# Feed-forward input through the 'A' bank, output and z transposes one slot sooner

## What is computed

```python
x = x + attn_a(_layernorm(x))   # 16 heads of 8, rotary, layer norm on q and k, softmax over all 256 keys
x = x + ffn(_layernorm(x))      # token-shift feed-forward
x = x + attn_b(_layernorm(x))   # windowed attention and one gradient step of a memory MLP
x = x + ffn(_layernorm(x))
```

```python
xr = mu_r * x + (1.0 - mu_r) * x_prev       # x_prev: x one token earlier
xk = mu_k * x + (1.0 - mu_k) * x_prev
r = sigmoid(xr @ W_r.T)
out = r * (square(relu(xk @ W_k.T)) @ W_v.T)
```

## Time and profile before

| | us |
|---|---|
| median of 3 runs | 1365.89 (1365.3 to 1366.46) |
| the profiled execution, time | 1367.37 |
| the profiled execution, span from first to last instruction | 1365.6 |
| TensorE busy | 1284.8 (94%) |
| VectorE busy | 1122.7 (82%) |
| ScalarE busy | 901.9 (66%) |
| GpSimd busy | 504.9 (37%) |

### The profile page before, as it was taken

One profiled execution on the slowest core, in us unless ns is written; L12 is line 12 of the kernel. 1 busy time (PEld: TensorE's weight loads), 2 busy tenths in 40 slices (PEclk: granted clock), 3 DMA queues, 4 the chain that ended last, 5 costly groups with the idle time before them and its releaser, 6 DMA issues.

```text
span 1365.6 us, 32982 instructions
## 1 busy us (share of the span) xinstructions
PE 1284.8 (94%) x10579; PEld 852.4 (62%) x10579; DVE 1122.7 (82%) x2849; ACT 901.9 (66%) x2504; POOL 504.9 (37%) x815
## 2 busy tenths in 40 slices
PE   7889999999999999888999999999999998999996
PEld 5445555555555555545566666666666665888885
DVE  5888999999999999876888888888888875778786
ACT  3278888888888888876565566556655653555563
POOL 5446666666666666533111111111111100232322
PEclk9999999999999999999999999999999999999998
DMA  2222332223333323210100010000000001232220
GB/s 80 77 76 81 82 79 76 73 78 80 82 91 103 99 69 84 67 51 17 32 28 29 28 49 28 30 28 28 27 30 25 20 17 41 79 87 82 85 86 27
DMA packets 101963, 79.61 MB, mean 58 GB/s; under 512 B 13780, under 2 KB 95124, under 8 KB 101796
## 3 DMA queue, kind: packets, MB, share of 16 engines
q1 hardware_dynamic: 100820, 76.99, 20.0%
q10 hardware_dynamic: 976, 0.54, 0.2%
HBM read 49.70 MB, written 27.79 MB: 57 GB/s over the span
## 4 chain that ended last, share of the span: by engine, by line
PE 49%; issue 1%; DVE 1%; ACT 1%; POOL 0%; POOLq 0%; DVEq 0%; ACTq 0%
PE b_psZ L1410 4%; PE b_psD L1331 4%; PE b_psZ L1342 4%; PE b_g L1394 4%; PE d_psO L1954 4%; PE b_g L1381 4%; PE d_psH L1946 4%; PE b_psM L1443 2%; PE b_psR L1387 2%; PE b_psL L1372 2%; PE b_psR L1403 2%; PE b_psD L1433 2%; PE b_psM L1455 1%; PE d_psG L1972 1%; PE d_psV L1985 1%
## 5 line engine op out<-in xcount | busy, mean ns | idle before, releaser
L790 DVE TENSOR_REDUCE a_MX<-a_psS 128x4 f32<-128x1024 f32 x248 | 303.2, 1223 | 44.6 <-PE a_psS L304 41.2
L591 ACT ACTIVATE a_PT<-a_psE 128x512 f32<-128x512 f32 x504 | 275.1, 604 | 59.3 <-PE a_psE L321 56.4
L1811 POOL TENSOR_TENSOR b_SWB<-b_b2col,b_SW 128x128 f32<-128x128 f32 x65 | 38.8, 597 | 346.2 <-ACT b_SW L1526 346.2
L335 PE MATMUL a_psV<-a_PT,a_VX 128*32 128x256 f32 x2048 | 137.0, 385 | 0.2 <-ACT a_PT L591 0.2
L1545 ACT ACTIVATE b_TH<-b_psZ 128x512 f32<-128x512 f32 x65 | 38.9, 598 | 128.7 <-PE b_psZ L1342 124.3
L304 PE MATMUL a_psS<-a_KS,a_QS 48*128 48x256 f16 x992 | 97.7, 275 | 22.1 <-DVE a_MX L790 20.6
L321 PE MATMUL a_psE<-a_QS,a_KS 50*128 50x256 bf16 x1008 | 97.5, 270 | 3.1 <-ACT a_PT L591 3.1
L1565 ACT ACTIVATE b_PR<-b_psL,b_mx 128x128 f32<-128x128 f32 x260 | 93.1, 369 | 0.9
L304 PEld LDWEIGHTS a_psS<-a_KS,a_QS 48*128 48x128 bf16 x992 | 29.1, 94 | 103.1 <-issue 48.2
L335 PEld LDWEIGHTS a_psV<-a_PT,a_VX 128*32 128x32 f32 x2048 | 53.4, 109 | 50.5 <-issue 27.5
L1693 DVE SCALAR_TENSOR_TENSOR b_HH<-b_TH,b_psZ 128x512 f32<-128x512 f32 x65 | 44.8, 689 | 44.1 <-ACT b_TH L1545 44.0
(11 more groups left out here) (298 smaller groups left out, 3426.4 us busy)
## 6 DMA issues: line engine op xcount, KB each, us to landing
a_KS<-kparts SPq DMA_DIRECT2D x63, 192.0 KB
a_QS<-qparts SPq DMA_DIRECT2D x126, 96.0 KB
qparts<-a_QP SPq DMA_DIRECT2D x64, 96.0 KB, 2.2
a_X<-x_in SPq DMA_DIRECT2D x32, 128.0 KB, 2.3
kparts<-a_KP SPq DMA_DIRECT2D x64, 64.0 KB, 2.1
x<-a_X SPq DMA_DIRECT2D x32, 128.0 KB, 1.8
b_X<-x SPq DMA_DIRECT2D x32, 128.0 KB, 2.2
zT<-b_XT SPq DMA_DIRECT2D x32, 128.0 KB, 1.7
```

Of the source, the lines that this page charges most:

```text
L335: mm = nc.tensor.matmul(psV[32 * h:32 * h + 32, 0:T], VX[:, b % UV, kt, at:at + 32], PT[:, gg, kt, h, :], start=(gg == 0 and kt == 0), sto ...
L591: nc.scalar.activation(PT[:, g % 2, :, h + s, :], shifted_bank(b, p, s), ACT.Exp).then_inc(S["exp"], 1)
L790: nc.vector.reduce_max(MX[:, b % 2, :].rearrange("q (s n) -> q s n", s=2)[:, :, 2 * p:2 * p + 2], score_banks(b, p)[:], AX.X).then_inc(S[" ...
```

## The change

Four things, all in the queues' order and in the bank used:

1. `fz_t` on TensorE writes `psA` instead of `psC` for elements b < B - 6 = 26, and ScalarE's copies read `psA` there. It waits for the readers of the centred q and k instead of for ON. The wait of `on_t` for the copies stays only where `psC` is still used. The K product, which overwrites `psA`, gets the wait for all four copies.
2. On ScalarE both pairs of copies stand in p3, one behind the other; `ot(c - 4, 0)` moves from p4 to p5, behind the exponentials of p5.
3. On TensorE `on_t` and `z_t` move from p5 to p4, behind `pv(.., 1)`. `ffn_kr` is split: the K product stands in p5 between `scores` and `shifted`, the R product behind `shifted`.
4. In p6 `out_proj` stands ahead of `hr_t` on TensorE, and `x1` ahead of `normed` on VectorE.

```diff
--- before.py
+++ after.py
@@ -424,7 +424,7 @@
 
         def on_t(b):
             wait(pe, "on", b)
-            if b < B - 1:
+            if B - 6 <= b - 1 < B - 2:
                 wait(pe, "fzT", b - 1, per=4)
             for t in range(NT):
                 mm = nc.tensor.transpose(psC[:, t * P:(t + 1) * P], ON[:, t, :], ident[:])
@@ -440,26 +440,32 @@
 
         def fz_t(b):
             wait(pe, "fz", b)
-            if b == B - 1:
+            if b < B - 6:
+                wait(pe, "square", b + 6)
+                wait(pe, "centred", b + 6)
+            elif b == B - 1:
                 wait(pe, "x1", b)
             elif b == B - 2:
                 wait(pe, "exp", B - 1, per=2 * NP)
             else:
                 wait(pe, "on", b + 1)
             for t in range(NT):
-                to = psE[0][:, 0, t * P:(t + 1) * P] if b == B - 2 else psC[:, t * P:(t + 1) * P]
+                to = (psE[0][:, 0, :] if b == B - 2 else psC if b >= B - 6 else psA)[:, t * P:(t + 1) * P]
                 mm = nc.tensor.transpose(to, FZ[:, t, :], ident[:])
             mm.then_inc(S["fzT_ps"], 1)
 
-        def ffn_kr(b):
+        def ffn_k(b):
             if b == 0:
                 pe.wait_ge(S["prep"], 3)
             wait(pe, "square", b + 6)
             wait(pe, "centred", b + 6)
+            wait(pe, "fzT", b, per=4)
             if b >= B - 6:
                 wait(pe, "gv", b - 1)
             wait(pe, "mixed", b, per=2, done=1)
             nc.tensor.matmul(psA[:, 0:T], wk_t[:], FX[:, 1, :], start=True, stop=True)
+
+        def ffn_r(b):
             wait(pe, "mixed", b, per=2)
             for t in range(NT):
                 mm = nc.tensor.matmul(psA[:, T + t * P:T + (t + 1) * P], FX[:, 0, t * P:(t + 1) * P], wr_t[:], start=True, stop=True)
@@ -477,6 +483,9 @@
                 if on(c - 2):
                     scores(c - 2, p)
                     keep_busy({2: 1, 3: 1}.get(c, 0), psV[:, 0:T])
+                if p == 5:
+                    if on(c - 6):
+                        ffn_k(c - 6)
                 if on(c - 4):
                     shifted(c - 4, p)
                 if p == 0:
@@ -502,20 +511,20 @@
                 if p == 4:
                     if on(c - 4):
                         pv(c - 4, 1)
-                if p == 5:
                     if on(c - 5):
                         on_t(c - 5)
                     if on(c + 1):
                         z_t(c + 1)
+                if p == 5:
                     if on(c - 6):
-                        ffn_kr(c - 6)
+                        ffn_r(c - 6)
                 if p == 6:
                     if on(c - 4):
                         pv(c - 4, 2)
+                    if on(c - 5):
+                        out_proj(c - 5)
                     if on(c):
                         hr_t(c)
-                    if on(c - 5):
-                        out_proj(c - 5)
                 if p == 7:
                     if on(c - 6):
                         ffn_v(c - 6)
@@ -557,7 +566,8 @@
             fz_t(B - 2)
             out_t(B - 1)
             yield B + 4, 1
-            ffn_kr(B - 2)
+            ffn_k(B - 2)
+            ffn_r(B - 2)
             on_t(B - 1)
             out_proj(B - 1)
             yield B + 4, 2
@@ -565,7 +575,8 @@
             yield B + 4, 3
             fz_t(B - 1)
             yield B + 4, 4
-            ffn_kr(B - 1)
+            ffn_k(B - 1)
+            ffn_r(B - 1)
             yield B + 4, 5
             ffn_v(B - 1)
             yield B + 4, 6
@@ -661,8 +672,9 @@
                 act.wait_ge(S["zeros"], 1)
             wait(act, "fzT_ps", b)
             wait(act, "mixed", b - 1, per=2)
-            nc.scalar.activation(FC[:, part, :], psC[:, 0:T], ACT.Copy, scale=vecs[:, 4 + part:5 + part]).then_inc(S["fzT"], 1)
-            nc.scalar.activation(FP[:, part, 1:T], psC[:, 0:T - 1], ACT.Copy, scale=past[:, part:part + 1]).then_inc(S["fzT"], 1)
+            src = psA if b < B - 6 else psC
+            nc.scalar.activation(FC[:, part, :], src[:, 0:T], ACT.Copy, scale=vecs[:, 4 + part:5 + part]).then_inc(S["fzT"], 1)
+            nc.scalar.activation(FP[:, part, 1:T], src[:, 0:T - 1], ACT.Copy, scale=past[:, part:part + 1]).then_inc(S["fzT"], 1)
 
         def ffn_kr(b):
             wait(act, "kr_ps", b)
@@ -687,12 +699,10 @@
                 if p == 3:
                     if 0 <= c - 6 < B - 4:
                         fz_t(c - 6, 1)
-                if p == 4:
-                    if 0 <= c - 6 < B - 4:
                         fz_t(c - 6, 0)
+                if p == 5:
                     if on(c - 4):
                         ot(c - 4, 0)
-                if p == 5:
                     if on(c - 5):
                         on_t(c - 5)
                     if on(c + 1):
@@ -948,6 +958,8 @@
                 if p == 6:
                     if on(c + 2):
                         sums(c + 2)
+                    if on(c - 5):
+                        x1(c - 5)
                     if on(c):
                         normed(c)
                 if p == 0:
@@ -960,9 +972,6 @@
                 if p == 3:
                     if B - 4 <= c - 6 < B:
                         fz_copies(c - 6)
-                if p == 6:
-                    if on(c - 5):
-                        x1(c - 5)
                 if p == 7:
                     if on(c - 6):
                         gv(c - 6)
```

## The result

| | before | after |
|---|---|---|
| median of 4 runs each, same chip, us | 1365.95 (1365.3 to 1366.46) | 1379.85 (1377.15 to 1380.62) |
| ratio, with its 95% interval | | 1.0091 [1.0075, 1.0108] |
| profiled execution: time, span | 1367.37, 1365.6 | 1380.19, 1378.4 |
| busy in the span: TensorE, VectorE | 1284.8, 1122.7 | 1306.8 (95%), 1134.5 (82%) |
| busy in the span: ScalarE, GpSimd | 901.9, 504.9 | 901.3 (65%), 502.6 (36%) |

The change makes the kernel slower: by 0.9% as a ratio, which is 12.4 us, or by the 13.9 us between the medians. The forecast was slower by 3.6 us; the time lies above the range, which ended at 1376.0. So the sign was right and the size was not.

A forecast was written before the change was run, and what follows sets the result against it. No engine has much room, so waits between engines decide. Later starts through p4 to p0 were to lengthen each period by 0.14 us, 26 x 0.14 = +3.6 us, giving 1369.5 us; range 1362.5 to 1376.0.

The forecast's parts named there:

- Copies, hand-over from the copies to the exponentials: ScalarE, p4: both copy pairs put the exponentials of p4 1.46 us behind the period's first copy, instead of 0.73.
- gate of ScalarE: Earliest start that the exponentials of p4 allow TensorE's shifted scores of p5: 242.55, 0.06 us behind their end.
- Transposes a slot sooner: TensorE, p4: two transposes cost 0.46, the return 0.05; scores of p5 start 1.95 us behind the first copy.
- stall of L430: TensorE's idle time ahead of transpose L430, waiting for ScalarE's copy FP: 28 times, 9.9 us in all; claimed gone.
- The K product: TensorE, p5, between scores and shifted scores: 0.32 + 0.44 + 0.05; shifted scores 0.15 us behind the gate of ScalarE.
- even rival: TensorE does not hold up the shifted scores of p5; the period doesn't move, 1365.9 us; chance 0.28.
- The OT copy: ScalarE, p5, behind the exponentials: lets the PV product of p6 start at 244.56, the shifted scores at 244.59.
- Projection ahead of the HX transposes: TensorE and VectorE, p6: x1 saves 0.33, a later transpose costs 0.49; maximum of p7 starts 0.14 us later.
- The second path: Exponentials of p6, KR, GpSimd's square, V product: scores of p0 at 248.74, the same time as by VectorE's maximum.
- Dearer hand-overs: Copies to PV product of p6: longer ScalarE-to-TensorE hand-overs and exponentials, period 0.40 us longer, 1376.3 us; chance 0.17.
- Faster: ScalarE does not hold the PV product of p6; period 0.20 us shorter, 1360.7 us; chance 0.15.
- The sum: Whole run: 26 periods x 0.14 = +3.6 us, first and last periods zero, carried to the median: 1369.5 us.

The follow-up runs named there:

- k_behind: Changed kernel with the K product behind the shifted scores of p5 instead of ahead; 1367.92 us, ratio to before 1.0007, period 18.14.
- k_ahead: Changed kernel with the K product ahead of the scores of p5, behind the two transposes; one execution, 1383.14 us, period 18.42.
- ot_back: Changed kernel with the OT copy alone put back in p4, ahead of the exponentials of p5; one execution, 1380.88 us, period 18.48.
- after_old_p6: Changed kernel with the old order in p6 (HX transposes ahead of the projection, QK ahead of x1); ratio to before 1.0069, period 18.38.
- split_copies: Changed kernel with K product behind shifted scores, OT copy and second copy pair in p4, old p6 order; ratio to before 1.0010, period 18.03.
- sum_later: Changed kernel with one wait more: GpSimd's second sum waits for VectorE's small step; ratio to before 1.0074, period 18.52.

## Why the prediction was right or wrong, point by point

- **Copies, hand-over from the copies to the exponentials.** 1.44 against 1.46. Right. The row's 0.365 a copy held: neighbours in after start 0.37, 0.36, 0.35 and 0.36 apart. The estimate of 0.40, worked out from the Trainium skill, page "ScalarE: Activation LUTs", section "What ACT_TABLE_LOAD costs", is too long here. The gate of ScalarE for the shifted scores of p5 was at 245.87 + 1.10 + 0.06 = 247.03; in k_behind, where only it decides, they start 0.06 behind the exponentials' end (246.76 + 1.10).
- **Transposes a slot sooner.** The stall of L430 went, as said. But scores of p5 came at 2.03, not 1.95: the two transposes and the return to the 48-row group took 246.46 - 245.87 = 0.59, not 0.51. This is the first mis-sized term, 0.08: L363 alone takes 0.31 to the scores, and 0.22 to the K product in k_ahead. The return costs 0.09. I had read 0.05, from four matmuls of another group (L465 against L412). The other 0.04 is L430, which takes 0.28 until L363 behind the PV product and took 0.24 behind idle time.
- **The K product.** The 0.32 behind the scores was right (246.46 to 246.78), so the even rival is out. The product itself took 0.63 until the shifted scores, not 0.44 + 0.05. This is the step that failed, by 0.14, the largest of the three terms that were too small. I priced it at the row where it stands behind L363, another 128-row group, though the change puts it between groups of 48 and 50 rows. Going in costs 0.10 and coming out 0.09: 0.63 there, 0.53 in k_ahead, 0.54 in k_behind (behind L321, ahead of L471), 0.44 between two 128-row groups. A row with the right neighbour was in the trace of before: two identical projections in a row, the first behind L321, take 0.53 and 0.43.

```profile
248.82 0.40 PE L321 MATMUL a_psE<-a_QS,a_KS 50*128 50x256 bf16 x4
249.15 0.70 PE L375 MATMUL a_psA<-a_ZT,a_wall 128*128 128x256 f32 x2
249.68 0.59 PE L376 MATMUL a_psA<-a_ZT,a_wall 128*128 128x256 f32 x2
250.11 0.27 PE L347 MATMUL a_psB<-a_ident,a_MX 128*32 128x128 f32 x1
```

- With 0.08 and 0.14 the K product holds the shifted scores for 0.38 beyond ScalarE's gate, not 0.15. That is 0.22 of the missing 0.27.
- **The OT copy.** I had it ready 0.03 before the shifted scores let the PV product go, 244.56 against 244.59. But I gave it the hand-over of 0.06; with the 0.15 that the trace also had, it decides, 249.20 + 0.15 = 249.35. Another 0.05, shown by ot_back (0.04). With 0.01 of the exponentials' delay and 0.01 of rounding the other way this makes up the 0.27.
- **Projection ahead of the HX transposes.** Price 0.14 predicted, 0.14 to 0.16 in three comparisons. The details were off and made up for each other: the projection takes 0.55 and not 0.49 until the transposes, now that it stands directly behind the PV product (the 0.49 was the row of the transposes in that place), and QK starts 0.63 behind the transposes, not 0.69. That VectorE idles before x1 was right (0.57). Before QK the profile shows no idle time, though QK starts 0.44 behind x1, and in before the maximum follows x1 by 0.33.
- **The second path**, by ScalarE, GpSimd and the V product, was to reach the scores of p0 together with VectorE's. It had 0.16 to spare in after: the V product starts at 7.83, and with 0.54 for it and for the next product that is 8.91, against 9.07. The term that was too long is that from ONT to the exponentials, 1.05 (249.07 to 250.12) and not 1.21. In after_old_p6, where the maximum of p7 comes 0.15 sooner, the scores of p0 do stand directly behind the two products, at 8.93. So that run could give back hardly more than its 0.14.
- **The rivals.** "Dearer hand-overs" gave the period almost exactly, +0.40, but by another mechanism: it took both exponential-to-TensorE hand-overs at 0.15, and they are 0.06 here (248.92 to 248.98). Its number is no credit to it. "Faster" asked that the exponentials of p5 start at FC + 2.84; they start at 3.41, and even in k_behind, where they no longer wait for the K product, they start at 3.02 (248.34 - 245.32).
- **The sum.** 26 x 0.41 = 10.7 where 3.6 stood. The remaining 3.2 of the 13.9 between the medians is not explained by the periods. The profiled executions put 1.8 into the opening, and one kernel's opening varies by more than that (100.41 and 96.97). Two executions of after and eight of before that had the same mean clock, 0.989, are 12.2 apart (1383.1 and 1370.9). Of what is left beyond the 10.7 I can't say whether the change has a part in it; the ratio of after built again, 1.0088, rests on 1368.01 for before and gives 12.0.
- **The range.** Its upper end left 10.7 us of slowdown out because the dearest case took dearer hand-overs and not a dearer K product; the two could have been added. The K product had been costed from one row, without the bound that the row above gives.
- **The signs.** The stall's end, the PV product 0.15 and 0.43 behind the OT copy and the exponentials, and VectorE's wait before x1 came as said. The shifted scores of p5 stood 0.95 behind the scores instead of 0.8, ScalarE idled 0.87 ahead of the exponentials of p5 instead of about 0.5, and the period was 18.52 and not 18.25.

Whether the product could be had between the scores and the shifted scores at less, with groups of equal row counts, wasn't tried.

## What to carry to other kernels

Price a moved group of matmuls by a row in which it, or its like, has the same neighbours as in its new place; the same instructions cost 0.44, 0.53 or 0.63 here, by what stood before and behind. A stall that is removed pays only if what is queued behind it has no longer way round: here the gain of 0.13 a period was there, and was spent four times over by two reorderings in the same slots, one of which (a product put between the two steps of a ring between engines) looked free because it filled TensorE's idle time. Take such a change apart edit by edit before judging it as a whole: two of its parts lose, and the rest is faster than both kernels.

## What the runs showed of the hardware

- A group of matmuls over 128 rows directly behind one over 48 or 50 rows takes 0.10 us longer until the next one starts, and a 48-row group behind it starts 0.09 later (0.63, 0.53 and 0.44 for the same two matmuls). I had expected 0.05 in all. The profile shows no idle time there; it stands as a longer duration. The 128-row groups are of 32-bit numbers and the 48- and 50-row ones of 16-bit numbers, so these rows don't tell the row count from the type. For going in, phase b of before does: four f32 matmuls over 128 rows take 0.54 until the next group behind f32 matmuls over 64 rows (L1455, below), and 0.43 behind f32 matmuls over 128 rows (L1403). For coming out no row separates the two. That a change of tiling mode makes TensorE drain is stated by the Trainium skill, page "TensorEngine Tiling (Array Packing)", section "Key Properties", without a figure. If a group over fewer rows counts as another mode, the rows agree with it; what happens inside the engine they can't show.

```profile
1001.46 1.02 PE L1342 MATMUL b_psZ<-b_w1f,b_XT 128*128 128x512 f32 x2
1002.32 0.60 PE L1403 MATMUL b_psR<-b_ident,b_PR 128*128 128x128 f32 x4
1002.75 0.27 PE L1354 MATMUL b_psM<-b_ident,b_ET 128*128 128x128 f32 x1
...
1006.91 1.05 PE L1372 MATMUL b_psL<-b_KT,b_QT 64*128 64x128 f32 x16
1007.90 0.71 PE L1455 MATMUL b_psM<-b_wf,b_XT 128*128 128x128 f32 x4
1008.44 1.02 PE L1331 MATMUL b_psD<-b_w,b_ET 128*128 128x512 f32 x2
```

- Hand-over from ScalarE to TensorE is 0.06 for the exponentials to the shifted scores, 0.15 for OT to the PV product, 0.26 for the last copy to the K product in split_copies. One figure for all of them doesn't fit. That the longer ones belong to lines with several waits is my reading and not tested.
- A small VectorE step took 0.66 us instead of 0.23 because GpSimd's sum was running (0.23 in all 32 once the sum waits, sum_later), with no effect on the period.
